# A projection of one fp32 matmul per tile, written as three fp32r matmuls of high and low parts

## What is computed

```python
def reference(x, adj, W, b):
    m, v = mean(x, -1), var(x, -1)
    h = maximum((x - m) / sqrt(v + 1e-5), 0)
    d = where(rowsum(adj) > 0, rowsum(adj) ** -0.5, 0)
    support = (d[:, None] * adj * d[None, :]) @ h
    return x + relu(support @ W + b)
```

## Time and profile before

| | |
|---|---|
| median of 3 runs | 416.89 us (416.85 to 418.31) |
| the profiled execution, own time | 419.11 us |
| its span in the trace | 417.3 us |
| PE busy | 393.9 us (94%) |
| DVE, ACT, POOL busy | 286.3 us, 281.3 us, 137.1 us |
| DMA | 147.39 MB, mean 353 GB/s |
| mean granted TensorE clock | 0.99 |

### The profile page before, as it was taken

The page is one execution under the profiler, slowest core; times in us unless marked ns, Lnnn a source line. Parts: engine busy times, 40 slices in busy tenths (PEclk is TensorE's granted clock), DMA queues, the critical chain, the costliest instruction groups (busy, mean ns, idle before and its releaser), DMA issues.

```text
span 417.3 us, 4994 instructions
## 1 busy us (share of the span) xinstructions
PE 393.9 (94%) x1760; PEld 326.9 (78%) x1760; DVE 286.3 (69%) x286; ACT 281.3 (67%) x253; POOL 137.1 (33%) x303
## 2 busy tenths in 40 slices
PE   2998999999999998599999999999999999997995
PEld 2887888888888876388888888888888888886884
DVE  6644878879696945928745596547846477749984
ACT  1899786959696878477655867487665877345542
POOL 3233535343133233013610354011810211635650
PEclk9999999999999999899999999999999999998999
DMA  8997999998989899999986999599994996296663
GB/s 322 422 418 311 426 419 422 381 426 342 426 342 428 337 408 424 395 418 423 421 371 223 404 426 423 205 354 413 425 421 146 390 425 277 97 393 234 205 227 155
DMA packets 22473, 147.39 MB, mean 353 GB/s; under 512 B 2608, under 2 KB 2864, under 8 KB 6064
## 3 DMA queue, kind: packets, MB, share of 16 engines
q1 hardware_dynamic: 22448, 147.07, 87.3%
HBM read 142.87 MB, written 4.19 MB: 352 GB/s over the span
## 4 chain that ended last, share of the span: by engine, by line
PE 84%; DMA 7%; DVE 3%; ACT 2%; issue 2%; SPq 0%; DVEq 0%; ACTq 0%
PE moved L696 18%; PE moved L697 18%; PE moved L698 18%; PE held L696 7%; PE held L697 7%; PE held L698 7%; DMA at<-in_adj_t 5%; PE held L666 4%; PE moved L666 2%; PE moved L650 2%; DMA nat<-in_adj 2%; ACT hi L343 1%; DVE acc L563 1%; PE moved L712 1%; DMA at<-in_x 1%
## 5 line engine op out<-in xcount | busy, mean ns | idle before, releaser
L696 PE MATMUL moved<-hi,G 128*128 128x512 f32 x384 | 151.2, 394 | 0.7 <-DVE acc L563 0.7
L697 PE MATMUL moved<-lo,G 128*128 128x512 f32 x384 | 149.9, 390 | 0.0
L698 PE MATMUL moved<-hi,G 128*128 128x512 f32 x384 | 149.7, 390 | 0.0
L335 ACT ACTIVATE nat<-nat 128x2048 f32<-128x2048 f32 x64 | 122.2, 1911 | 6.8 <-DMA nat<-in_adj 6.8
L548 DVE TENSOR_TENSOR lo<-at,hi 128x2048 fp32r<-128x2048 f32 x40 | 91.8, 2295 | 48.6 <-ACT hi L343 48.6
L343 ACT CAST hi<-at 128x2048 fp32r<-128x2048 f32 x40 | 76.4, 1909 | 66.7 <-PE moved L698 47.9
L563 DVE TENSOR_TENSOR acc<-moved,acc 128x1024 f32<-128x1024 f32 x60 | 73.3, 1222 | 51.3 <-PE moved L698 51.3
L696 PEld LDWEIGHTS moved<-hi,G 128*128 128x128 f32 x384 | 72.4, 189 | 15.9 <-DVE acc L563 1.1
L698 PEld LDWEIGHTS moved<-hi,G 128*128 128x128 f32 x384 | 72.3, 188 | 15.2
L697 PEld LDWEIGHTS moved<-lo,G 128*128 128x128 f32 x384 | 72.4, 189 | 14.8
L459 POOL TENSOR_TENSOR row_sum<-part 128x1 f32<-128x1 f32 x32 | 9.8, 306 | 203.9 <-ACT nat L335 203.9
(11 more groups left out here) (54 smaller groups left out, 261.7 us busy)
## 6 DMA issues: line engine op xcount, KB each, us to landing
nat<-in_adj SPq DMA_DIRECT2D x64, 1024.0 KB, 10.3
at<-in_adj_t SPq DMA_DIRECT2D x64, 1024.0 KB, 10.5
nat<-in_x_t SPq DMA_DIRECT2D x6, 512.0 KB, 3.6
out<-nat SPq DMA_DIRECT2D x5, 512.0 KB, 3.7
at<-in_x SPq DMA_DIRECT2D x4, 512.0 KB, 5.0
turned<-in_x SPq DMA_DIRECT2D x3, 512.0 KB, 3.9
turned<-in_x_t SPq DMA_DIRECT2D x2, 512.0 KB, 5.2
out<-turned SPq DMA_DIRECT2D x2, 512.0 KB, 3.8
```

The lines of the kernel that those rows point to most:

```text
L335: nc.scalar.activation(nat[m % LN][:, :], nat[m % LN][:, :], ACT.Copy, accum_out=part[:, m // 2, m % 2:m % 2 + 1]).then_inc(nat_summed, 1)
L696: nc.tensor.matmul(into[:, f, :], big, hi[g % RING][:, t, :], start=begins, stop=False)
L697: nc.tensor.matmul(into[:, f, :], big, lo[g % RING][:, t, :], start=False, stop=False)
L698: mm = nc.tensor.matmul(into[:, f, :], small, hi[g % RING][:, t, :], start=False, stop=ends)
```

## The change

W and the transposed chunk are each split into a high part (rounded to fp32r by ACT) and a low part (the rest, by DVE), and the product of the two is the sum of three fp32r matmuls: high by high, high by low, low by high. So there are 24 matmuls of 256 columns per chunk. The two parts of the transposed chunk lie in the place in `G` that this chunk's own product takes later; W is loaded into the first part of `acc`, which is free then. ACT has a copy of W ahead of its first work, and one wait less in `take_turned`. DVE has one subtraction for W (`rest_of_w`, 512 elements in each partition) and one for each chunk (`rest_of_turned`, 1024 elements, read from PSUM), and its order at the start is another.

```diff
+        w_sb = acc[:, 0, 0, :].rearrange("p (f n) -> p f n", n=D)
+
+        def hT(c, a):
+
+            flat = G[:, BW * c:BW * (c + 1), :, :].rearrange("p t a f -> p (t a f)")
+            return flat[:, a * FD * PW:(a + 1) * FD * PW].rearrange("p (f r) -> p f r", r=PW)
...
             def take_turned(c):
                 act.wait_ge(h_turned, c + 1)
-                if 2 <= c < AHEAD:
-                    act.wait_ge(hW_done, c - 1)
-                nc.scalar.copy(hT(c), pair_of(("turn", c))[:, :, :]).then_inc(hT_ready, 1)
+                nc.scalar.copy(hT(c, 0), pair_of(("turn", c))[:, :, :]).then_inc(hT_hi_made, 1)
...
+            act.wait_ge(w_landed, DMA)
+            nc.scalar.copy(w_hi[:, :, :], w_sb).then_inc(w_hi_made, 1)
             take_turned(0)
...
+            def rest_of_w():
+                dve.wait_ge(w_hi_made, 1)
+                nc.vector.tensor_tensor(out=w_lo[:, :, :], in0=w_sb, in1=w_hi[:, :, :].bitcast(F32),
+                                        op=ALU.subtract).then_inc(w_ready, 1)
+
+            def rest_of_turned(c):
+                dve.wait_ge(hT_hi_made, c + 1)
+                nc.vector.tensor_tensor(out=hT(c, 1), in0=pair_of(("turn", c))[:, :, :], in1=hT(c, 0).bitcast(F32),
+                                        op=ALU.subtract).then_inc(hT_ready, 1)
...
             centre(0)
+            rest_of_w()
             centre(1)
+            rest_of_turned(0)
             take_stats(2)
+            centre(2)
+            rest_of_turned(1)
             take_stats(3)
-            centre(2)
             centre(3)
+            rest_of_turned(2)
+            rest_of_raw(0)
             take_stats(4)
-            rest_of_raw(0)
             centre(4)
+            rest_of_turned(3)
             rest_of_raw(1)
+            rest_of_turned(4)
             rest_of_raw(2)
...
                 if c is not None and q == 4:
                     centre(c)
+                if c is not None and q == 5:
+                    rest_of_turned(c)
...
                         for f in range(FD):
-                            mm = nc.tensor.matmul(chunk_product(c)[:, a, t * D:(t + 1) * D],
-                                                  hT(c)[:, f, tile * P:(tile + 1) * P], w_sb[:, f, :],
-                                                  start=(f == 0), stop=(f == FD - 1))
+                            nc.tensor.matmul(into, hT(c, 0)[:, f, rows], w_hi[:, f, :], start=(f == 0), stop=False)
+                            nc.tensor.matmul(into, hT(c, 0)[:, f, rows], w_lo[:, f, :], start=False, stop=False)
+                            mm = nc.tensor.matmul(into, hT(c, 1)[:, f, rows], w_hi[:, f, :], start=False,
+                                                  stop=(f == FD - 1))
...
-            pe.wait_ge(w_landed, DMA)
+            pe.wait_ge(w_ready, 1)
             project(0)
```

More of the change, by code:

```diff
@@ L125, in sem @@
             return ctx.enter_context(nc.semaphore(name))
-        w_sb = sb("w_sb", [P, FD, D])
+        w_hi = sb("w_hi", [P, FD, D], F32R)
+        w_lo = sb("w_lo", [P, FD, D], F32R)
         b_sb = sb("b_sb", [P, FD])
@@ L158, in build @@
         turned = [sb(f"turned{e}", [P, BW * D]) for e in range(2)]
-        def hT(c):
-            return turned[c % 2][:, :].rearrange("p (f r) -> p f r", r=PW)
+        w_sb = acc[:, 0, 0, :].rearrange("p (f n) -> p f n", n=D)
+        def hT(c, a):
+            flat = G[:, BW * c:BW * (c + 1), :, :].rearrange("p t a f -> p (t a f)")
+            return flat[:, a * FD * PW:(a + 1) * FD * PW].rearrange("p (f r) -> p f r", r=PW)
         def hW(c):
@@ L212, in build @@
         h_turned = sem("h_turned")
+        hT_hi_made = sem("hT_hi_made")
         hT_ready = sem("hT_ready")
+        w_hi_made = sem("w_hi_made")
+        w_ready = sem("w_ready")
         hW_done = sem("hW_done")
@@ L290, in _ @@
             load_x(1)
-            sp.dma_start(w_sb[:, :, :], w.rearrange("(f p) n -> p f n", p=P)).then_inc(w_landed, DMA)
+            sp.dma_start(w_sb, w.rearrange("(f p) n -> p f n", p=P)).then_inc(w_landed, DMA)
             load_x(2)
@@ L664, in project @@
                         tile = half * a + t
+                        into = chunk_product(c)[:, a, t * D:(t + 1) * D]
+                        rows = slice(tile * P, (tile + 1) * P)
                         for f in range(FD):
-                            mm = nc.tensor.matmul(chunk_product(c)[:, a, t * D:(t + 1) * D],
-                                                  hT(c)[:, f, tile * P:(tile + 1) * P], w_sb[:, f, :],
-                                                  start=(f == 0), stop=(f == FD - 1))
+                            nc.tensor.matmul(into, hT(c, 0)[:, f, rows], w_hi[:, f, :], start=(f == 0), stop=False)
+                            nc.tensor.matmul(into, hT(c, 0)[:, f, rows], w_lo[:, f, :], start=False, stop=False)
+                            mm = nc.tensor.matmul(into, hT(c, 1)[:, f, rows], w_hi[:, f, :], start=False,
+                                                  stop=(f == FD - 1))
                 mm.then_inc(hW_done, 1)
```

## The result

| | before | after |
|---|---|---|
| median of 5 runs | 417.86 us (416.85 to 419.26) | 421.18 us (420.28 to 422.77) |
| ratio to before | | 1.0087, 95% interval 1.005 to 1.0125 |
| profiled execution, own time (span) | 419.11 (417.3) us | 420.28 (418.5) us |

The change makes the kernel 3.3 us slower. The forecast was 417.6 us in a range up to 420.6, and no change as the likeliest. The two profiled executions mislead a little when set side by side: that of before is among its slower runs, that of after is its fastest. All ratios here compare fast runs alone, which leaves out two runs of e2 (425.4 and 426.3 us), one of e5 (450.6) and one of e6 (2290.1).

The account below looks back on a forecast made before the run. PE was taken to bound the main loop, PE and ACT together the start-up. Plus 2.6 us at the start and minus 1.9 us in the loop gave +0.7 on the 416.89 us median: 417.6 us, range 415.9 to 420.6.

Parts of the forecast that it names:

- The plus 2.6 us at the start: Before the main loop: DVE's new order delays POOL and ACT, so the loop starts at 36.1 instead of 33.5 us.
- the walk: Start-up, step by step through DVE, POOL and ACT queues: mean_of(4) at 23.5, s of tile 1 at 31.0, loop at 36.1.
- with 2.8 us per projection: PE at the start: five projections of 2.8 us each, ending at 33.4, leaving 2.7 us of PE free.
- The forecast case without a fall of the clock: Whole kernel: the start and loop terms alone, 417.6 us, own range 416.4 to 418.7; chance 0.53.
- this rival: After PE's idleness before the main loop, the granted clock falls: 1.6 us lost, 419.2 us in all; chance 0.28.
- the gap of its own forecast: Just before the main loop: PE idle from 33.4 to 36.1 us.
- its argument against the fall: At make_G before the longest wait: a PE wait of about 3 us was not followed by a slow stretch.
- The minus 1.9 us in the loop: Three main-loop projections: 24 matmuls of 0.117 us replace 3.45 us of fp32, 0.65 us less per chunk.
- The slow-matmul rival: All projections: 256-column fp32r matmuls at 0.222 us, about 431 us; a middle way 419.5 to 426; chance 0.13.
- a late pair at panel 6: Main loop: DVE's new subtraction fits with 0.4 us margin; without cover, at most 1.2 us more per chunk.
- The forecast's own +0.7: Whole kernel: net of the start's plus 2.6 us and the loop's minus 1.9 us.
- The rival that the start doesn't wait: At the start: nothing lost if mean_of(4) starts before about 20.7; 415.0 us, at most 413.6; chance 0.06.

Follow-up runs that it names:

- e2: Against the kernel before: three-part product and new order only for the five chunks before the main loop, loop chunks in fp32; ratio 1.0113.
- e5: The whole change with mean_of(4) on POOL moved behind scale_of(0) and rstd_of(1); ratio to the kernel before 1.0004.
- e6: The kernel before with 26 transpositions of ident added on idle PE ahead of turn(0); ratio to the kernel before 0.9976.
- e7: The whole change with 26 transpositions of ident added on idle PE ahead of turn(0); ratio to the kernel before 1.0101.
- e9: The change as made, run once more with nothing altered; ratio to the kernel before 1.0102.
- e3: Against the kernel before: three-part product for the three loop chunks only, start in fp32 and old order with W's parts made there; 414.58 us, ratio 0.9937.
- e10: The whole change with 24 transpositions of ident on PE between project(4) and the main loop; ratio to the kernel before 1.0048.
- e4: The whole change with another order on DVE at the start, statistics of chunks moved earlier, POOL's order kept; ratio to the kernel before 0.9984.
- e1: The kernel before, unchanged, run again to see its scatter; ratio to the kernel before 1.0010.
- e11: The whole change with another DVE order at the start and 26 transpositions on PE ahead of turn(0); ratio to the kernel before 0.9962.

## Why the prediction was wrong, point by point

**The plus 2.6 us at the start: the mechanism was right, the size was not.** Each station of the walk is in the trace: the statistics of chunk 4 behind `rest_of_raw(0)` (23.19, forecast 22.0), `mean_of(4)` (24.74, forecast 23.5), the s of tile 1 (32.6, forecast 31.0), ACT's idleness between the halves of slot 0 (2.88 us, forecast over 2). But the main loop came at 37.7, not 36.1. The step of the prediction that failed is "with 2.8 us per projection", taken for project(0) too, while the 33.5 of before contains a first projection that ran partly at 1.2 GHz. The timeline of PE in the kernel before would have told it: its first projection took 4.47 us, the second 3.62. In the profile of the change the first one took 4.6 us and not 2.8.

```profile
11.52 4.47 PE L666 MATMUL held<-w_sb,turned 128*128 128x256 f32 x16
...
16.70 3.62 PE L666 MATMUL held<-w_sb,turned 128*128 128x256 f32 x16
```

I set a start at full clock against a start at partly low clock, and that makes the difference look about a microsecond smaller. Where both are equal (e6 and e7) it is 3.7 us; where the change's clock rose at 11.5 us (e9) the walk came true station by station (`mean_of(4)` 23.36, s of tile 1 31.25) and main was at 36.4, close to my 36.1, and the fp32 start of e3, whose clock rose at 12.1, had 33.1. In the profile of the change the low level lasted until 15.8 us; project(0) ended 1.0 us later than before, `round_raw(0)` moved from 16.02 to 17.07 on ACT and the copy of chunk 2 with it, and `rest_of_turned(2)` had to wait 1.41 us for that. That makes 1.2 of the 1.6 us; the rest came on POOL, where the walk took its lengths from the kernel before and the piece of 0.67 us added 0.48.

**The forecast case without a fall of the clock, 0.53 against 0.28: the odds were the wrong way round.** Of the four profiled executions in which PE waits 2.9 us or more before the main loop (the change, e2, e7, e9) three have half clock right behind it, and none of the others, which wait 1.0 to 1.3 us, has. In the means the change loses 6.0 us (its five runs) to 6.9 (e9) to the low level, and the kernel before 4.8 to 5.7; against the runs of before on its own chip e9 has 1.7 more. Filling the gap takes the excess away (e10), 2.3 us against e9. So this rival is a part of the mean: about +1.7 us, give or take 1.5. That is near the 1.6 it was given, but one fall cost 1.7 us (e7) or 3.4 (e2, e9). The prediction names the gap of its own forecast as the cause and still weighs the fall as an alternative; it belonged into the sum, as its price times its chance. And its argument against the fall was half a reading: it names the first wait for `make_G`, 2.98 us, which had none, and not the second, of 3.54 us, behind which half clock ran for 3.4 us (0.93 in the window from 160 us). Of the three waits over 2 us that the kernel before has after its first matmul, two were followed by half clock.

**The minus 1.9 us in the loop.** Right in kind: 0.12 us per matmul (forecast 0.117), 0.57 us per chunk, 1.7 in all, and e3 shows it as time. One matmul with the load of its 128 x 128 weights takes 0.120 us, so the load hides behind 256 columns. The slow-matmul rival falls. So does a late pair at panel 6: no wait. The stalls of PE later on are a little shorter than before (6.2 and 1.6 us, where the earlier trace rows had 6.5 and 2.4). The span of the profiled execution grew by only 1.2 us, and that is in part luck with the clock. By position the change was 4.2 us behind at main, 4.0 at the end of the second wait for `make_G` (177.52 against 173.50), 2.6 at the end of the late stall (380.80 against 378.17), and 1.2 at the end: the last 1.4 us came where before ran 3.4 us at half clock and the change did not.

**Sum.** +3.5 (3.3 to 3.7 at like clock) + 1.7 - 1.7 = +3.5 us, against +3.3 measured. That it meets so well is partly luck, with a clock term so roughly known. The forecast's own +0.7 was 417.6 only because the median of three runs it was set against was 416.89; over the later runs before stands near 417.7. So of the 3.6 us between 417.6 and 421.18 the start has about 0.9, the fallen clock about 1.7, the loop 0.2, and the base 0.8.

**The rival that the start doesn't wait** was wrong for the change as made. Its condition is met in e4 and e5, where `mean_of(4)` starts at 18.4, or stands behind the first scale, and ACT does not wait for s. Its time is not: it said 415.0 and a main loop no later than before, and they had 417.6 and 418.1 us by their medians and main at 35.3 and 34.6. PE and ACT then wait for each other and for DVE, and the start still costs about what the loop gives, 1.5 us in e5 against the 33.1 of e3 at nearly the same clock.

**Still open.** Why e3 gains 3.1 us by its median and not 1.7: its runs lose 3.6 us to the low level and those of before 4.8, a difference that eight runs do not hold apart from nothing. The profiles point at the late stall: it is 0.9 us in e3, without half clock behind it, and 2.4 and 2.1 in before and e1, with 3.4 us of half clock. Of the thirteen profiles the eight with 0.8 to 1.8 us there have no such fall, and four of the five with 1.9 to 2.4 have it. Whether the three-part product shortens the stall, or only the shift in time, was not tried.

**Why e10's and e2's main loops came late** is in their traces. In both the `row_pow` of tile 1 on POOL (31.31 in e10, 31.74 in e2) began while DVE computed the low part of slot 0, and took 1.45 us in place of 0.57; another piece had lost 0.2 us against `centre(4)`. In the change, e7 and e9 the piece after it met the same DVE instruction and took 0.67 in place of 0.19. So where POOL's chain falls against one DVE instruction moved main by 0.5 us in three profiles and by 0.9 and more in two.

## What to carry to other kernels

When a step is given more pieces on a side engine, walk every in-order queue that the piece passes, and ask which small instruction of a third engine now stands in front of others: here one mean on POOL held two scales, and moving it down by two lines gave back nearly 1%. Take an edit only where the engine that it relieves is the bound: in the loop the three-part product is worth 1.7 us, at the start it cost 3.5, and the kernel with it in the loop alone is the better one (0.9937, and 0.9907 with PE warmed). And where a forecast opens a gap on PE like this one (2.9 to 3.6 us here, with 1.7 or 3.4 us lost behind it in three profiles of four), put the low clock into the sum with its chance, and compare two starts only at the same clock.

## What the runs showed of the hardware

- The same program scatters by about 4 us (415.0 to 420.2 for the kernel before), with mean granted clocks of 0.982 to 0.996. Part of it is where the low stretches fall.
- Where full clock begins differed: about 13.1 us in before, 11.5 and 15.8 us in two executions of the same changed kernel. It moved the first main matmul by 1.3 us (36.4 and 37.7).
- At the two waits for `make_G` (2.3 to 4.1 us each) every one of the thirteen profiles has a stretch of half clock, of 3.4, 6.8 or 10.2 us. The same kernel does not always have the same: 10.2 us in the profile of the change, 3.4 in e9.
- A small instruction of POOL that begins while DVE runs `SCALAR_TENSOR_TENSOR` on two operands in SBUF (L563) often lasts until DVE is through, or longer: 0.67 us in place of 0.19 (the change, e7, e9), and 1.45 in place of 0.57 (e2, e10). While DVE subtracts from PSUM (L534, L540) the same instructions keep their lengths (0.19 and 0.57 us).
- 26 transpositions of 128 columns on an idle PE from 1.67 us on brought full clock at 5.0 to 5.7 us, but it did not always last: in e11 the spacing went back to the low level at 12.5 us, after PE had idled twice for over a microsecond. The Trainium skill (TensorE: Matmul & The Clock Gate, Part 4: PE-mode transpose) says that the full clock does not engage in transpose mode; these fp32 transpositions brought it, and the measurement decides.
- An fp32r matmul of 256 columns follows the next in 0.120 us and one of 512 in 0.227; at the low level 0.213 and 0.427. What is spent beyond the columns (0.107 and 0.213 us at 2.4 GHz) appears at the high level only, 13 to 14 ns each. By the Trainium skill (TensorE: Matmul & The Clock Gate, Back-to-back issue gap) the isolated gap at the high level is the columns at 2.4 GHz plus 2.5 ns, 109 ns for 256; this stream of loads and matmuls has 120, and the measurement decides.
